# An attention kernel on one core: its rough scores in five rounds per body instead of six, with new places in TensorE's and VectorE's orders

## The reference, cut to what matters

```python
xn = layernorm(x)                                  # x: 8 x 512 tokens x 128
qkv = xn @ W_qkv                                   # 32 query heads, 16 key/value heads of 64
scores = q @ k.T / 8 + slope[head] * (pos_k - pos_q)   # causal
s = softmax(scores) @ v  -> @ W_out                # attention
g = silu(experts(xn))                              # 2 of 8 experts per token, width 512
out = x + s * g
```

## Time and profile before

| | |
|---|---|
| median of 3 runs | 1212.18 us (1210.99 to 1213.15) |
| span of the profiled execution, first to last instruction | 1211.8 us |
| PE busy | 93% of the span |
| DVE, ACT, POOL busy | 82%, 77%, 73% |
| attention, first half | about 40 to 540 us |
| expert part | about 540 to 700 us |
| attention, second half | about 700 to 1212 us |

### The profile page before, as it was taken

The page is one execution under the profiler, slowest core; times in us unless marked ns, Lnnn a source line. Parts: engine busy times, 40 slices in busy tenths (PEclk is TensorE's granted clock), DMA queues, the critical chain, the costliest instruction groups (busy, mean ns, idle before and its releaser), DMA issues.

```text
span 1211.8 us, 51694 instructions
## 1 busy us (share of the span) xinstructions
PE 1128.9 (93%) x16970; PEld 834.2 (69%) x16970; DVE 988.1 (82%) x3099; ACT 936.6 (77%) x1835; POOL 888.1 (73%) x1064
## 2 busy tenths in 40 slices
PE   2668999999999999999999998999999999999996
PEld 1446767677777777777888766677777777777775
DVE  7687898888888888885777867788888888888883
ACT  3547878888888888886666677788888888888884
POOL 6069989898888888885000077788888888888896
PEclk9989999999999999999999999999999999999998
DMA  8424765556555555555335337655555555555553
GB/s 259 161 54 105 135 125 133 128 131 134 128 130 127 127 129 127 130 133 99 86 84 123 76 79 163 129 128 122 123 123 122 121 122 125 125 121 122 122 125 74
DMA packets 267956, 148.74 MB, mean 123 GB/s; under 512 B 173154, under 2 KB 256450, under 8 KB 267204
## 3 DMA queue, kind: packets, MB, share of 16 engines
q1 hardware_dynamic: 263476, 138.72, 51.8%
q0 software_dynamic: 4096, 8.40, 2.5%
q10 hardware_dynamic: 272, 0.13, 0.0%
HBM read 15.76 MB, written 16.78 MB: 27 GB/s over the span
## 4 chain that ended last, share of the span: by engine, by line
PE 63%; POOL 16%; issue 6%; DVE 3%; ACT 2%; SPq 2%; DMA 2%; POOLq 0%; ACTq 0%; DVEq 0%
POOL t_lo L829 11%; PE ps L998 10%; PE ps L904 7%; PE ps L970 6%; PE ps L905 6%; PE ps L906 6%; PE outs L1030 5%; PE ps L1002 5%; PE outs L1034 5%; PE outs L1032 4%; PE ps L999 3%; PE ps L1007 2%; ACT stage L1299 2%; PE outs L905 1%; PE outs L904 1%
## 5 line engine op out<-in xcount | busy, mean ns | idle before, releaser
L829 POOL TENSOR_TENSOR t_lo<-stage 128x512 f16<-128x512 f32 x640 | 651.8, 1037 | 121.5 <-ACT stage L1299 120.0
L1592 DVE CUSTOM_DVE_ANT_0 stage<-ps,kmask 128x512 bf16<-128x512 f32 (+3 forms) x1024 | 451.4, 488 | 113.5 <-PE ps L970 98.6
L1299 ACT ACTIVATE stage<-ps,slope 128x512 f32<-128x512 f32 (+1 forms) x768 | 439.5, 617 | 91.5 <-PE ps L1007 79.5
L998 PE MATMUL ps<-q_st,k_st 128*128 128x256 f16 (+3 forms) x1024 | 299.8, 303 | 9.2 <-issue 5.0
L1030 PE MATMUL outs<-v_sp,stage 128*128 128x65 f16 x2560 | 264.6, 195 | 7.9 <-POOL t_lo L829 6.4
L1032 PE MATMUL outs<-v_sp,stage 128*128 128x64 f16 x2560 | 263.3, 194 | 0.0
L1034 PE MATMUL outs<-v_sp,t_lo 128*128 128x65 f16 x2560 | 263.1, 194 | 0.0
L1030 PEld LDWEIGHTS outs<-v_sp,stage 128*128 128x128 bf16 x2560 | 235.4, 98 | 32.1 <-issue 14.2
L1032 PEld LDWEIGHTS outs<-v_sp,stage 128*128 128x128 bf16 x2560 | 235.7, 99 | 0.0
L1034 PEld LDWEIGHTS outs<-v_sp,t_lo 128*128 128x128 f16 x2560 | 235.4, 98 | 0.0
L999 PE MATMUL ps<-q_st,k_st 128*128 128x128 f16 x1024 | 223.9, 219 | 0.0
(11 more groups left out here) (218 smaller groups left out, 2672.3 us busy)
## 6 DMA issues: line engine op xcount, KB each, us to landing
q_st<-stage SPq DMA_DIRECT2D x256, 128.0 KB, 2.4
k_st<-stage SPq DMA_DIRECT2D x128, 128.0 KB
q_st<-stage SPq DMA_DIRECT2D x256, 64.0 KB, 2.0
k_st<-stage SPq DMA_DIRECT2D x128, 64.0 KB
slot_y<-stage SPq DMA_DIRECT2D x40, 128.0 KB, 2.1
X<-in_L_attn_inputs SPq DMA_DIRECT2D x8, 512.0 KB, 6.6
slot_x<-att SPq DMA_DIRECT2D x2, 2048.0 KB, 8.8
wx_raw<-in_L_ffn_w SPq DMA_DIRECT2D x64, 64.0 KB
```

Source lines behind the costliest of these rows:

```text
L829: pool.tensor_tensor(t_lo[r], t_p[r], upper(t_p[r]), ALU.subtract).then_inc(s[f"lo{u % NG}"], 1)
L998: pe.matmul(d, k[:, 0, at], q[:, 0, seen], start=(c0 == 0), stop=False, skip_group_check=True)
L1299: e = act.activation(t_p[r][:, c0:c1], S_ps[u % 2][:, c0:c1], ACT.Exp, scale=slope[:, bass.ds(pair_index(n) * 2 * SLOTS + sl * 2 + h, 1)])
L1592: ins = dve.tensor_tensor_reduce(junk[h][:, c0:c0 + w], M_ps[h][:, c0:c0 + w], kmask[:, SEQ - w:SEQ], -1.0 / 1024, 3e38, ALU.add, ALU.min, ...
```

## The change

- `ROUNDS` holds five rounds for a body, as (slot, i, first column), and one of them has tiles of both slots: tile 1 of slot 0 in columns 0 to 255 and tile 1 of slot 1 in columns 256 to 511. All five rounds have 512 columns per h.
- M0 to M4 and B0 to B9 replace M0 to M5 and B0 to B11. The tiles, their matmuls (16 a body) and their reductions (16 a body) are the same. The mixed round waits for the queries and keys of both slots.
- One semaphore `rough` and two `peak` semaphores replace two and four. `q_hi` of a slot waits for the last round of the body before that reads that slot (`LAST_ROUND`: round 2 for slot 0, round 4 for slot 1).
- New places. First half, PE: S0, M1, P9, S1, S2, Q1, V0, M2, S3, S4, K0, S5, P0, M3, P1, P2, S6, S7, P3, P4, M4, Q0, S8, S9, O0, C0, M0, P5 to P8. DVE: O0, B2, B3, N1, Q1, B4, A1, B5, V0, B6, K0, B7, N0, B8, B9, Q0, A0, B0, B1 (before: O0, B2, B3, N1, B4, B5, Q1, A1, B6, B7, V0, K0, B8, B9, N0, B10, B11, Q0, A0, B0, B1). The lists of ACT, POOL and SP stay.

```diff
-ROUNDS = [[(3, 0)], [(0, 0), (2, 128)], [(1, 0)]]
+ROUNDS = [[(0, 3, 0)], [(0, 0, 0), (0, 2, 128)], [(0, 1, 0), (1, 1, 256)], [(1, 3, 0)], [(1, 0, 0), (1, 2, 128)]]
+LAST_ROUND = [max(r for r, parts in enumerate(ROUNDS) if sl in [part[0] for part in parts]) for sl in range(2)]
...
         "DVE": [
-            ("B2", 1, 1), ("B3", 1, 6), ("N1", -1, 11), ("B4", 1, 18), ("B5", 1, 20), ("Q1", 1, 23), ("A1", -1, 30),
-            ("B6", 1, 35), ("B7", 1, 39), ("K0", 2, 43), ("V0", 1, 48), ("B8", 1, 54), ("B9", 1, 59), ("N0", 0, 64),
-            ("B10", 1, 70), ("B11", 1, 73), ("Q0", 2, 75), ("A0", 0, 80), ("B0", 2, 87), ("B1", 2, 92),
+            ("B2", 1, 1), ("B3", 1, 6), ("N1", -1, 11), ("Q1", 1, 18), ("B4", 1, 25), ("A1", -1, 30),
+            ("B5", 1, 35), ("K0", 2, 43), ("B6", 1, 45), ("V0", 1, 48), ("B7", 1, 54), ("N0", 0, 64),
+            ("B8", 1, 66), ("B9", 1, 72), ("Q0", 2, 75), ("A0", 0, 80), ("B0", 2, 87), ("B1", 2, 92),
...
-            ("S0", 0, 0), ("P9", -1, 3), ("S1", 0, 5), ("Q1", 1, 9), ("M2", 1, 13), ("S2", 0, 15), ("V0", 1, 18),
-            ("S3", 0, 23), ("M3", 1, 26), ("S4", 0, 28), ("K0", 2, 32), ("S5", 0, 36), ("P0", 0, 39), ("P1", 0, 42),
-            ("P2", 0, 44), ("P3", 0, 47), ("M4", 1, 49), ("S6", 0, 52), ("S7", 0, 55), ("P4", 0, 59), ("Q0", 2, 61),
-            ("M5", 1, 66), ("S8", 0, 67), ("S9", 0, 70), ("O0", -2, 74), ("M0", 2, 83), ("C0", 1, 85),
+            ("S0", 0, 0), ("P9", -1, 3), ("S1", 0, 5), ("Q1", 1, 9), ("S2", 0, 15), ("V0", 1, 18), ("M2", 1, 20),
+            ("S3", 0, 23), ("S4", 0, 28), ("K0", 2, 32), ("S5", 0, 36), ("P0", 0, 39), ("M3", 1, 40), ("P1", 0, 42),
+            ("P2", 0, 44), ("P3", 0, 47), ("S6", 0, 52), ("S7", 0, 55), ("P4", 0, 59), ("M4", 1, 60), ("Q0", 2, 61), ("S8", 0, 67), ("S9", 0, 70), ("O0", -2, 74), ("M0", 2, 83), ("C0", 1, 85),
...
-                need(act, f"rough{sl}", n * NR)
+                need(act, "rough", (n - 1) * NR + LAST_ROUND[sl] + 1)
...
-                sl, r, h = round_of(j)
-                dve.wait_ge(s[f"rough{sl}"], n * NR + r + 1)
+                r, h = divmod(j, 2)
+                dve.wait_ge(s["rough"], n * NR + r + 1)
```

More of the change, by code:

```diff
@@ L289, in build @@
                 s[f"{step}{u}"] = sem(f"s_{step}{u}")
[L290 to L293, removed]
+        s["rough"] = sem("s_rough")
+        for h in range(2):
+            s[f"peak{h}"] = sem(f"s_peak{h}")
         block = ctx.enter_context(nc.Block())
@@ L332, in build @@
         FIRST_ONES = {"SP": [("A1", HALF), ("A1", HALF + 1), ("A0", HALF + 2), ("A1", HALF + 2)],
-                      "DVE": [("B1", 0), ("B3", 0), ("B5", 0), ("B7", 0), ("B9", 0), ("B11", 0),
-                              ("B3", 1), ("B5", 1), ("B7", 1), ("B9", 1), ("N0", 0), ("B11", 1),
+                      "DVE": [("B1", 0), ("B2", 0), ("B3", 0), ("B5", 0), ("B7", 0), ("B9", 0),
+                              ("B2", 1), ("B3", 1), ("B5", 1), ("B7", 1), ("N0", 0), ("B9", 1),
                               ("N0", 5), ("N0", 8), ("A1", HALF - 1)],
@@ L339, in build @@
         CHOICES = 6
-        FILL_AT = {"M0": 84, "B0": 85, "B1": 85, "M1": 95, "M2": 18, "B4": 18, "B5": 18, "M3": 35, "B6": 35, "B7": 35, "M4": 51,
-                   "B8": 51, "B9": 51, "M5": 68, "B10": 68, "B11": 68}
+        FILL_AT = {"M0": 84, "B0": 85, "B1": 85, "M1": 95, "M2": 22, "B4": 22, "B5": 22, "M3": 42, "B6": 42, "B7": 42, "M4": 60,
+                   "B8": 60, "B9": 60}
         def go_ahead(engine_name, tasks, lo, hi):
@@ L495, in x_bank @@
             return ps[4] if q == 0 else ps[q % 4]
-        def round_of(j):
-            sl, j = divmod(j, NR * 2)
-            return sl, j // 2, j % 2
         def v_bank():
@@ L951, in vals, with rough @@
                 mm.then_inc(s["vmm"], 1)
[L953 to L957, removed]
+            def rough(n, par, r):
+                for sl in sorted({part[0] for part in ROUNDS[r]}):
+                    need(pe, f"qh{sl}", n + 1)
+                    need(pe, f"kst{sl}", (n + 1) * 32)
                 for h in range(2):
[L959 to L963, removed]
+                    need(pe, f"peak{h}", n * NR + r)
+                if isinstance(n, int) and n == 0 and r == 0:
                     pe.wait_ge(s["xlo"], NB)
-                for i, c0 in ROUNDS[r]:
+                for sl, i, c0 in ROUNDS[r]:
                     w = (i + 1) * P
@@ L971, in rough @@
                                        k_st[par][sl][head, 0, 0:w], start=True, stop=True)
-                mm.then_inc(s[f"rough{sl}"], 1)
+                mm.then_inc(s["rough"], 1)
             def turn_shifts(n, par, _):
                 bank_free(n, "C0")
-                for sl in range(SLOTS):
-                    for h in range(2):
-                        need(pe, f"peak{sl}{h}", (n + 1) * NR)
+                for h in range(2):
+                    need(pe, f"peak{h}", (n + 1) * NR)
                 for i in range(QT):
@@ L1194, in _ @@
                         step_of(i_, c, g)
-            for sl in range(SLOTS):
-                for h in range(2):
-                    pe.wait_ge(s[f"peak{sl}{h}"], HALF * NR)
+            for h in range(2):
+                pe.wait_ge(s[f"peak{h}"], HALF * NR)
             for sl in range(SLOTS):
@@ L1582, in peaks @@
             def peaks(n, par, j):
-                sl, r, h = round_of(j)
-                dve.wait_ge(s[f"rough{sl}"], n * NR + r + 1)
+                r, h = divmod(j, 2)
+                dve.wait_ge(s["rough"], n * NR + r + 1)
                 dve.nop(nofuse=True)
-                if j < 2:
+                if r == 0:
                     need(dve, "turnc", n - UNROLL + 1)
                     dve.nop(nofuse=True)
-                for i, c0 in ROUNDS[r]:
+                for sl, i, c0 in ROUNDS[r]:
                     w = (i + 1) * P
@@ L1594, in peaks @@
                         ALU.add, ALU.min, spread[par][:, i, SHIFT[sl][h]:SHIFT[sl][h] + 1])
-                ins.then_inc(s[f"peak{sl}{h}"], 1)
+                ins.then_inc(s[f"peak{h}"], 1)
             def q_lo(n, _, sl):
```

## The result

The changed kernel takes 1230.5 us (median; 1228.1 to 1234.0), the kernel before 1212.6 beside it: a ratio of 1.0157, 95% interval 1.0133 to 1.0181. It is 18 to 19 us slower. The forecast was 1212.9 with a range from 1201 to 1220.

What follows compares the result with a forecast made beforehand. PE was taken as the bound. First half +5.7 us (M3's stall beyond the saving), second half -4.6, expert part -0.4, total +0.7 on 1211.8 plus 0.4 around the span: 1212.9 us, range 1201 to 1220.

Steps and rivals of the forecast that it cites:

- 0.20 us per body from the merged round: Rough rounds on PE: five 512-column rounds cost 2.10 us per body, against 2.30 before.
- third rival: Merging saves nothing: four matmuls of 256 cost as two separate rounds; 1223.5 us, chance 0.05.
- PE side: First half, when PE wants M3: P0 at 5.73 us after M1 with M2 0.11 longer, M3 at 6.19.
- Elsewhere: Other steps, lists, semaphores and q_hi's wait cost nothing; start 0, expert part -0.4 us.
- M3's stall of 0.36 to 0.47: First half: DVE's chain through Q1 and B5 lets M3 start at 6.55 us, PE wants it at 6.19.
- First half +0.22 a window: First half's steady windows: M3's stall less the spared round, 26 x 0.22 = +5.7 us.
- Second half -0.17: Second half: M3 has no wait, by 0.05 us, 0.03 allowed before P5; 27 x -0.17 = -4.6 us.
- C0 level with Q0: First half: PE reaches C0 3.41 us after P4, DVE needs 3.42 for Q0's result; no cost, no slack.
- Semaphores and q_hi's own wait at nothing: q_hi's wait for the last round reading its slot costs nothing, as those rounds end most of a window earlier.
- the second half stalls as well: Second rival: the 0.05 us margin there fails; with 0.25 lost per window 1219 us, chance 0.13.
- The sign that was to tell them apart: PE idle on peaks rises from 10.1 us by about 10 more, at M3, in the first half only.
- first rival: The whole saving comes: B5 arrives in time in the first half too; 1201.2 us, chance 0.22.

Runs made afterwards that it cites:

- run 9: run 3 with, in the first half, Q1 ahead of S2 on PE and E2 on ACT, M2 behind S3, M3 behind P1: 1208.9 us, ratio 0.9945.
- run 1: Changed kernel with a rough round waiting first for peaks and keys, last for the queries' high part: 1218.3 us, ratio 1.0043.
- run 2: Changed kernel with M2 alone later on PE, behind S4 in the first half and S3 in the second: 1226.9 us, ratio 1.0119.
- run 7: Changed kernel with Q1 sooner in the first half, ahead of S2 on PE and E2 on ACT: 1226.9 us, ratio 1.0103.
- run 8: The merge without new places: five rounds, M0 to M4 and B0 to B9 at the old kernel's places: 1316.3 us, ratio 1.0846.
- run 6: run 5 with C0 behind M0 on PE in the first half: 1222.1 us, ratio 1.0065.
- run 4: Six rounds and orders of the kernel before, on the changed kernel's semaphores and q_hi wait: 1212.5 us, ratio 1.0002.
- run 3: Changed kernel with M2 and M3 later on PE, and on DVE A1 ahead of B4, K0 ahead of B6: 1211.2 us, ratio 0.9990.
- run 5: run 3 with K0 behind S5 on PE in the first half and queries waited for last: 1221.6 us, ratio 1.0057.
- run 10: run 9 with the queries waited for last in a rough round: 1213.2 us, ratio 0.9971.

## Why the prediction was wrong

- **What bounds it.** PE, as said; the loss is idle time of PE.
- **0.20 us per body from the merged round: right.** The mixed round takes 0.32 or 0.33 to the next start, as M1 does, and the windows of run 9, where no round waits, are 0.15 to 0.18 shorter than before. The third rival, and with it the Trainium skill's 60 cycles for each matmul ("TensorEngine Tiling (Array Packing)", "Instruction Overhead"), would have had run 9 no faster than before; it is.
- **The step that failed: M2 was given no wait at all.** "PE side" counted M2 only as 0.11 us longer and went on to M3. Under "Elsewhere" the prediction looked at q_hi's wait for the rounds, and not at the mixed round's wait for q_hi of slot 1, though the change says that it waits for both. Its own numbers held the answer: ACT's part starts 2.78 us after M1 and can't come sooner, and with its own lower bounds (0.69 for the instruction, 0.15 for the signal) M2 can't start before 3.62, while PE is there at 3.1. With the 1.15 us measured, it is 3.93; M2 starts at 3.94. So PE waits 0.80 us where the prediction had 0. Runs 1, 2, 7 and 8 move this wait or its size each time.
- **M3's stall of 0.36 to 0.47, first half: right in its chain, hidden in the result.** Once M2 is late, PE comes to M3 2.89 after it, while DVE lets it start 2.75 after it, so M3 has no wait. Run 1 has DVE's side at 6.51 (predicted 6.55), and run 2 has the links behind A1 and B5.
- **First half +0.22 a window: measured +0.5 to +0.6.** M2's wait goes beyond what M3's chain would have cost. In run 1, where the two are level, the window is 0.31 longer than before, so the chain alone comes to about +0.3 (an estimate from that run) and M2's wait adds some 0.3 to it.
- **Second half -0.17: measured +0.08.** M2's 0.23 was missing. M3 has no wait, also not in run 1, where M2 waits for 0.1 us at most and the window is 0.13 shorter than before. C0 and P5 cost nothing there.
- **C0 level with Q0: +0.09** in the first half, small; run 6 got 0.06 of it back in the loop.
- **Semaphores and q_hi's own wait at nothing: right** (run 4).
- **Rivals and signs.** None of the rivals was the mechanism. The second ("the second half stalls as well") comes nearest in its effect, but by another wait, and it left the first half as it was. The sign that was to tell them apart failed too: PE's wait for peaks went from 10.1 to 12.8 us over the whole run and not up by 10, and M3 doesn't wait in the first half; yet the first rival doesn't hold, since its wait stands at M2. PE's wait for ACT's queries went from 4.5 to 16.6 us:

```profile
PE ps L962 <- ACT stage L1230: 16.6, 19, 2.8
PE ps L962 <- DVE spread L1582: 12.8, 12, 3.3
```

## What to carry to other kernels

When tiles of two producers share one round, the round starts with the later of them: list every wait of the merged step, find when each producer ends relative to the step's old place, and only then count what the merge spares. A saving of 0.2 us per window on the engine that is full is worth a new order of the others: of the seven further orders tried with five rounds (runs 2, 3 and 5 to 9), one was faster than both kernels (run 9, and by less with the other order of waits, run 10), and each of the others kept a wait or turned a wait that was removed into the next one (K0's bank, S5's exponential, M3's peaks). Put the wait that is satisfied last at the end of the step's list, but measure it: it gave 14 us where the step was waiting and cost 3 where it wasn't. And look behind the wait that you remove: here M3's chain stood 0.3 us behind M2's wait, so half of the loss in the first half's windows would have stayed.

## What the runs showed of the hardware beyond that

- From the start of ACT's 512-column instruction (0.69 us) to the start of the matmuls that wait for it pass 1.13 to 1.15 us in three kernels (after, runs 7 and 8), and 0.83 to 0.84 in run 1, where no other wait stands behind that one. From DVE's last read to the waiting round it is 0.23 to 0.24 (run 2).
- One list of instructions ran in more than one rhythm: the second half's windows took 15.53 us after the changed first half and 15.76 after that of run 7, with the same lists from there on, by one trace of each.
